# The first expert tile ahead of the transposed scores in odd slots of attention

## What is computed

```python
x = layernorm(x + attn(x, x, x, causal=True))
x = layernorm(x + attn(x, ctx, ctx, causal=False))
# moe: topw, topi = top_k(softmax(x @ rw + rb), 2); topw = softmax(topw)
h = gelu(einsum('td,edf->etf', xf, w1) + b1)     # 128 -> 512
eo = einsum('etf,efd->etd', h, w2) + b2          # 512 -> 128
x = layernorm(x + einsum('td,te->td', eo, combine))
```

## Time and profile before

| what | value |
|---|---|
| median of 3 runs | 810.45 us (806.59 to 812.8) |
| profiled execution, its own time | 811.17 us |
| its span | 809.4 us |
| mean granted TensorE clock | 0.876 |
| PE busy | 593.2 us (73%) |
| DVE busy | 484.9 us (60%) |
| ACT busy | 452.9 us (56%) |
| POOL busy | 390.1 us (48%) |

### The profile page before, as it was taken

One profiled execution on the slowest core, in us unless ns is written; L12 is line 12 of the kernel. 1 busy time (PEld: TensorE's weight loads), 2 busy tenths in 40 slices (PEclk: granted clock), 3 DMA queues, 4 the chain that ended last, 5 costly groups with the idle time before them and its releaser, 6 DMA issues. The chain is left out here.

```text
span 809.4 us, 21265 instructions
## 1 busy us (share of the span) xinstructions
PE 593.2 (73%) x7870; PEld 468.5 (58%) x7870; DVE 484.9 (60%) x1319; ACT 452.9 (56%) x824; POOL 390.1 (48%) x603
## 2 busy tenths in 40 slices
PE   2676777767667798878988988787686776889900
PEld 1344445545444576665776766566576676778900
DVE  4455877777786677787875778855445540320241
ACT  1324553445333489977997889577567462443200
POOL 7122243333356344426854654685445674611575
PEclk9967887798868799998999999799899797999965
DMA  4352555833223555553755666355564476987311
GB/s 111 104 172 63 150 177 160 273 92 86 70 75 100 171 161 166 144 164 113 223 153 165 189 181 191 115 162 160 157 207 152 134 246 192 294 261 237 124 33 33
DMA packets 139398, 124.65 MB, mean 154 GB/s; under 512 B 12224, under 2 KB 121296, under 8 KB 139296
## 3 DMA queue, kind: packets, MB, share of 16 engines
q1 hardware_dynamic: 134496, 113.06, 46.7%
q0 software_dynamic: 4800, 10.23, 4.3%
HBM read 86.81 MB, written 38.54 MB: 155 GB/s over the span
## 5 line engine op out<-in xcount | busy, mean ns | idle before, releaser
L1064 DVE TENSOR_REDUCE row_max<-bank 128x16 bf16<-128x1024 f32 x64 | 78.3, 1223 | 78.1 <-PE bank L1464 77.4
L760 POOL TENSOR_TENSOR prob_lo<-probT,prob_hi 128x384 f16<-128x384 f32 x64 | 69.3, 1083 | 91.4 <-ACT prob_hi L874 91.0
L1512 PE MATMUL bank<-consts,o_n 128*128 128x64 f32 x256 | 46.7, 311 | 80.0 <-DVE o_n L1083 70.4
L1591 PE MATMUL bank<-w_in,w_hl 128*128 128x128 f32 x704 | 103.7, 293 | 0.0
L1512 PEld LDWEIGHTS bank<-consts,o_n 128*128 128x128 f32 x256 | 38.4, 215 | 94.0 <-issue 68.8
L871 ACT ACTIVATE probT<-bank 128x1024 f32<-128x1024 f32 x64 | 65.6, 1024 | 47.3 <-PE bank L1488 46.7
L783 POOL DMA_INDIRECT w_hl<-ys,pos x60 | 59.1, 985 | 67.6 <-DMA ys<-w_hl 42.9
L1591 PEld LDWEIGHTS bank<-w_in,w_hl 128*128 128x128 f32 x704 | 91.1, 202 | 0.3
L746 POOL TENSOR_TENSOR veps<-mv,eps 128x1 f32<-128x1 f32 x64 | 14.6, 228 | 136.6 <-DVE mv L1102 136.6
L1057 DVE TENSOR_TENSOR prob_lo<-probT,prob_hi 128x640 f16<-128x640 f32 x64 | 62.3, 973 | 25.5 <-ACT prob_hi L874 25.5
L1577 PE MATMUL bank<-xT,w_in 128*128 128x128 f16 x1056 | 76.3, 224 | 0.0
(11 more groups left out here) (171 smaller groups left out, 1574.7 us busy)
## 6 DMA issues: line engine op xcount, KB each, us to landing
w_in<-w_scr SPq DMA_DIRECT2D x96, 512.0 KB, 3.8
q_scr<-q_hl SPq DMA_DIRECT2D x64, 128.0 KB, 2.0
k_scr<-k_hl SPq DMA_DIRECT2D x64, 128.0 KB, 2.3
q_st<-q_scr SPq DMA_DIRECT2D x32, 256.0 KB, 3.7
k_all<-k_scr SPq DMA_DIRECT2D x128, 64.0 KB, 2.1
xs_tile<-xs SPq DMA_DIRECT2D x42, 128.0 KB, 3.7
ys<-w_hl SPq DMA_DIRECT2D x42, 128.0 KB, 2.2
xs<-xs_tile SPq DMA_DIRECT2D x3, 1472.0 KB, 6.8
```

What stands on the lines that cost most here:

```text
L760: pool.tensor_tensor(p_lo[u.buf][:, h, :], probT[u.buf][:, h, :], p_hi[u.buf][:, h, :], ALU.subtract).then_inc(lo_second[u.kind], 1)
L1064: dve.reduce_max(row_max[u.buf][:, :], bank[:, SC:SC + 2, :].rearrange("p a (h k) -> p (a h) k", k=S), AX.X).then_inc(max_done[a], 1)
L1512: last = pe.matmul(turned_o[:, 64 * b:64 * b + 64], o_n[u.buf][:, b, :, :, :].rearrange("p c a d -> p (c a d)"), consts[:, C_DELTA:C_TRI], ...
L1591: last = pe.matmul(expert_y(x), hid[x.par][:, c, :], w2_t[x.wb][:, c, :], start=False, stop=c == FC - 1, skip_group_check=True)
```

## The change

In slots with an odd number, below `ATTENTION_END` and with a tile (`tile_leads`), TensorE now writes the scores of this unit first, then transposes the next tile and runs the first layer of the slot's first tile, and only then writes the transposed scores. On ScalarE the copy of the turned tile and gelu stand ahead of the exponentials, while the copy of the earlier tile's result, now `result_step`, stays behind them. Even slots, second tiles and the tail keep their order. VectorE, GpSimd and SyncE are untouched.

```diff
+def tile_leads(slot):
+
+    return slot % 2 == 1 and slot < ATTENTION_END and bool(tiles_in(slot))
...
                 if y := x.near(1):
                     copy_turned(y)
                 gelu(x)
+
+            def result_step(x):
                 if y := x.near(-1):
                     copy_y(y)
...
+                if tile_leads(g):
+                    tile_step(tiles[0])
                 if u := unit_at(g - 1):
                     exps(u, same_buffers(g - 1))
+                if tiles and not tile_leads(g):
+                    tile_step(tiles[0])
                 for x in tiles[:1]:
-                    tile_step(x)
+                    result_step(x)
...
                 for x in tiles[1:]:
                     tile_step(x)
+                    result_step(x)
...
+            def tile_in(x):
+                if y := x.near(1):
+                    turn_tile(y)
+                up(x)
...
-                if u := unit_at(g - 1):
-                    scores_T(g, u)
-                if u := unit_at(g):
-                    scores(g, u)
-                for x in tiles[:1]:
-                    if y := x.near(1):
-                        turn_tile(y)
-                    up(x)
+                if tile_leads(g):
+                    if u := unit_at(g):
+                        scores(g, u)
+                    tile_in(tiles[0])
+                    if u := unit_at(g - 1):
+                        scores_T(g, u)
+                else:
+                    if u := unit_at(g - 1):
+                        scores_T(g, u)
+                    if u := unit_at(g):
+                        scores(g, u)
+                    for x in tiles[:1]:
+                        tile_in(x)
```

## The result

The changed kernel takes 823.8 us in the median of four runs (819.5 to 826.1), against 811.5 us for the kernel before on the same chip: 1.014 times as long, 95% interval 1.010 to 1.019. The profiled execution, the fastest of the four, took 819.53 us for a span of 817.7, 8.3 more than the span of before.

The account below looks back on a forecast made before the run. It took a loop through ScalarE and TensorE as the bound, VectorE having little slack. Pairs +0.8, two-tile slots +1.5 and slot 33 +0.3 made +2.6, taken as +3: 814 us against 813.5, range 800 to 824.

Parts of the forecast that it names:

- These now come earlier: VectorE's maxima, said to come earlier after the change; an argument against low parts slowing to 1.54 us as at 315.32.
- E to O, cross units: From an even slot's exponential to the next odd slot's, cross attention: 9.3 us where 7.53 were, plus 1.8.
- E to O, self units: From an even slot's exponential to the next odd slot's, self attention: 9.1 us where 7.10 were, plus 2.0.
- O to E: From an odd slot's exponential to the next even slot's: 6.0 us, minus 1.9; with the mask 6.3, minus 1.7.
- The chain of 3.85 us: VectorE in odd slots, low parts then outputs: o_n ends 3.85 us after the exponential, and the turn of o waits.
- Two-tile slots: Five odd slots with exponentials and two tiles (51, 53, 55, 67, 71): about +0.3 us each, +1.5 together.
- routing: Slots 41, 43, 57 and 59, where VectorE's routing was said to lie over the shift: 0.
- the pair 32, 33: Slot 33 had no load ahead of its exponential: some +2 us, of which its O to E gives 1.7 back, +0.3.
- the chain rival: VectorE's low parts slow down in the 14 counted pairs, 0.72 us each, +10 us: 824 us, chance 0.16.
- Loads as the path: Rival: each of the 18 removed table loads comes off the time, -23.1 us, 788 us; chance 0.10.
- The clock: Rival: TensorE's longer gap before even slots' turn of o lowers its clock, up to +26 us, 840 us; chance 0.06.
- E to O under 8.5 or O to E above 7: Sign that the prediction is wrong: E to O stays under 8.5 us, or O to E stays above 7.

Follow-up runs that it names:

- the kernels without switches: Tanh in place of gelu, one table load left: kernel before with it 796.69 us (0.982), changed kernel with it 807.6 us (0.995).
- that reordering on VectorE: VectorE's outputs of the unit before last ahead of the last unit's low parts, everywhere: kernel before 793.3 us (0.976), changed kernel 791.55 us (0.974).
- the kernel with ScalarE's part alone: Changed kernel with TensorE back in the old order; in odd slots copy and gelu stay ahead of the exponentials: 861.26 us (1.057).

## Why the prediction was right or wrong

**What bounds the kernel.** Right as far as it went: with all but one load gone the kernel before gains 15 of 104 us, so ScalarE was full, but not what set the time alone. That VectorE has "little slack" was the right warning, and I didn't follow it into the even slots. "These now come earlier", said of the maxima, holds for the odd slots, where the scores moved to the front; in the even ones it is the exponential that comes earlier.

**E to O, cross units.** 9.3 us predicted, 9.49 measured in slots 34 and 46. My 0.50 for gelu was the time to the start of an overlapping copy; a load doesn't overlap, and gelu to load took 0.62 (312.04 to 312.66). With four pairs that is half a microsecond.

**E to O, self units: the term that failed.** 9.1 predicted, 9.96 to 11.00 measured in slots 36, 44 and 48. The sum began with "turn of o 4.34 after the exponential", a duration that the earlier trace rows show for a slot whose exponential waits for a load (4.35 in slot 36 of before). Taking the load away moved the exponential toward the maxima, and the turn came at 5.49. Put 5.49 for 4.34 and 0.62 for 0.50 into the sum and it gives 10.3, which is what slot 36 measured. Over the four self pairs this half came out at +11.4 us for +8 predicted. Two of the four hold something else besides: in slot 48, whose turn came at +6.21, the clock was 0.58 over 406.69 to 410.20, and in slot 60, which holds two tiles, the turn came at +8.63 behind a copy of ScalarE and not behind o_n.

**O to E.** 5.93 to 6.07 and 6.29 to 6.30 where 6.0 and 6.3 were predicted, except 6.84 in slot 39, where the clock fell. The chain of 3.85 us to the end of o_n was right to the hundredth in slot 37. The values were right and the gain was too large by 0.7 in slots 45 and 61: there before had 7.27 and 7.32 us, not the 8.01 of slot 37, which I had generalised. That is 1.4 us of the miss.

**Two-tile slots, routing, the pair 32, 33.** Predicted +1.5, 0 and +0.3; measured +0.4 (slots 50 to 55) and +1.9 (from slot 64), +0.2, and -0.2. The slots 64 to 66, left at 0, took 28.21 us instead of 24.08, at a mean clock of 0.83 instead of 0.93, of which the slots behind them gave 2.3 back. Within the routing the zero is a sum of +2.0, -2.1, -1.4 and +1.8 for four pairs, right by compensation.

**The sum.** +2.6 predicted and taken as +3; +9.8 in the stretch, +8.3 in the span, +12.3 between the medians. The span lies just inside the forecast's own bounds of -3 to +9, the medians and the stretch outside. Single pairs were off by up to 2 us, where the bounds allowed for 0.4. The 823.8 us lie 0.2 us inside the range of 800 to 824, whose upper end was the price of the chain rival. That is luck: the rival's price came from low parts slowed in the odd slots, where they weren't. What was right was the direction and the half in the odd slots; what was wrong was that the even slots' turn of o keeps its distance from an exponential that comes earlier.

**The rivals.** Loads as the path: refuted, and by the kernels without switches far off (15 us for 81 loads, where the rival had 23.1 for 18). VectorE's chain costing more gave 824, which is the time measured, but not by its mechanism: in odd slots the low parts took 0.81 to 0.83 us, under the 1.1 from which it was to decide. The price arose in even slots. What made low parts slow there is what the rival named, GpSimd's half having started first: GpSimd ran from 322.26 for 1.15 us, and VectorE's low parts, issued at 322.55, took 1.54, ending 0.68 after it; max_diag at 306.02, begun inside GpSimd's 0.91 us from 305.68, took 1.12 instead of 0.69.

```profile
322.26 1.15 POOL L765 TENSOR_TENSOR prob_lo<-probT,prob_hi 128x384 f16<-128x384 f32 x1 [0.60 <-ACT prob_hi L879]
```

The Trainium skill, SBUF — State Buffer, section Who interferes with whom, describes an exclusive lock between the two engines when a VectorE operation has both inputs in SBUF and the GpSimd operation reads SBUF. By that rule, the trace agrees but for 0.14 us: VectorE ended 0.68 and 0.55 us after GpSimd did, where alone it takes 0.82 and 0.69.

**The clock.** I gave it 0.06 because a gap of 2.01 us had left the clock alone. Gaps of 1.82 us were followed by a lower clock in slots 39, 47 and 63 (0.50 over 560.30 to 562.30), and one of 1.81 in slot 35 wasn't. Nor was the longest of them, in slot 61; the clock stayed at 1.00 to the end of the slot and beyond:

```profile
540.22 0.63 PE L1524 MATMUL bank<-consts,o_n 128*128 128x64 f32 x4 [2.42 <-DVE o_n L1095]
```

The fall cost about 0.9 us in slot 39 (6.84 against 5.93), and the mean over the stretch stayed at 0.95, so the rival as priced, +26, is refuted. The length of a gap alone doesn't decide; what does stays open and wasn't tried.

**Profile after.** Loads 64, ScalarE's busy time -20.3 us (23 said; the durations in its timelines add up to 486.1 and 462.9 us, 23.2 apart, but the page counts time in which two of them overlap once), the wait for o_n behind an odd exponential 1.55 to 1.82 us in slots 35 to 49 (1 to 1.6 said). The wait of the turn at 371.11, which was to stay at about 3 us, fell to 1.55 (373.00), while that behind slot 42 rose from 0.68 to 2.22 (361.93): VectorE's routing shifted against the slots. The sign "E to O under 8.5 or O to E above 7" was not met; it guarded against an error in the other direction only.

## What to carry to other kernels

A duration measured from an event holds only while what stands ahead of that event stays: when a wait or a load is taken from one engine, its successors start earlier and meet the other engines at another point of their orders, so list for each neighbour what it is doing at the new time. A queue whose order is fixed should be checked for work that a waiting engine doesn't need standing ahead of what it does need: that reordering on VectorE gave the kernel before 19 us, most of them ahead of the tiles, while the reordering of the tile that started the study cost 12 with VectorE's old order and nothing with its new one. And the value of a removed stall is found by removing all stalls of its kind once: 81 loads of 1.28 us were worth 15 us.

## What was unexpected of the hardware

The granted clock fell from 1.00 to the 1.2 GHz level after gaps of 1.82 us in three slots, and stayed after the same gap in a fourth and after 2.42 us in a fifth. Before the fall in slot 39 the DMA engines were busy for 0.72 of the time. In the kernel with ScalarE's part alone the granted clock was 0.65 to 0.73 in nine of the twelve odd slots from 41 to 63. VectorE's slowdown beside GpSimd isn't proportional: 1.54 instead of 0.82 us and 1.12 instead of 0.69, in both cases what was left of GpSimd's operation and then its own time less 0.14. It holds the other way round: in slot 35 of after VectorE's low parts began first (299.70, 0.83 us) and GpSimd's, begun at 299.75, took 1.55 us, where 0.91 is its time in slot 36, in which it began first.
